# A chunked delta rule: zero rows under its 32-row operands, another order of its first products, its staging in three pieces

## What is computed

```python
H, DK, DV = (6, 32, 64)
beta = jax.nn.sigmoid(x @ Wb.T)
g = -jnp.exp(A_log) * jax.nn.softplus(x @ Wa.T + dt_bias)
q = l2norm(q) * DK ** (-0.5)
k = l2norm(k)

def step(S, inp):
    qt, kt, vt, gt, bt = inp
    S = S * jnp.exp(gt)[..., None, None]
    v_new = vt - jnp.einsum('bhk,bhkv->bhv', kt, S)
    S = S + bt[..., None, None] * (kt[..., :, None] * v_new[..., None, :])
    o = jnp.einsum('bhk,bhkv->bhv', qt, S)
    return (S, o)
_, o = jax.lax.scan(step, S0, (tm(q), tm(k), tm(v), tm(g), tm(beta)))
```

## Time and profile before

| | us |
|---|---|
| median of 3 runs | 3966.03 |
| lowest and highest run | 3959.83 and 3974.03 |
| the profiled execution | 3965.95 |
| its span in the trace | 3964.2 |
| mean granted TensorE clock | 0.933 |
| busy: PE, PEld | 3390.4 (86%), 2670.8 (67%) |
| busy: DVE, ACT, POOL | 2470.6 (62%), 1958.4 (49%), 1665.7 (42%) |
| `l2_delta_chunks` in the span | from 2142.8 to about 2523 |

### The profile page before, as it was taken

The page is one execution under the profiler, slowest core; times in us unless marked ns, Lnnn a source line. Parts: engine busy times, 40 slices in busy tenths (PEclk is TensorE's granted clock), DMA queues, the critical chain, the costliest instruction groups (busy, mean ns, idle before and its releaser), DMA issues. The chain is left out here.

```text
span 3964.2 us, 59001 instructions
## 1 busy us (share of the span) xinstructions
PE 3390.4 (86%) x18336; PEld 2670.8 (67%) x18336; DVE 2470.6 (62%) x4855; ACT 1958.4 (49%) x3947; POOL 1665.7 (42%) x1286
## 2 busy tenths in 40 slices
PE   5788698579888888879986999788888887998979
PEld 4566586158566666658874999656666666887868
DVE  4687544955577777775446444467777776545554
ACT  3777434333466666664333222256666664333333
POOL 1666221832466666642211433066666662221211
PEclk8899899999899999999997898799999998999989
DMA  2000232323110110003310000010000001332222
GB/s 79 18 29 2 76 110 64 133 95 108 46 29 25 25 29 23 19 19 119 111 62 5 1 1 1 34 41 23 23 23 25 25 16 61 114 109 85 80 88 75
DMA packets 81058, 203.12 MB, mean 51 GB/s; under 512 B 16923, under 2 KB 20123, under 8 KB 80662
## 3 DMA queue, kind: packets, MB, share of 16 engines
q1 hardware_dynamic: 80774, 201.26, 16.2%
q10 hardware_dynamic: 144, 0.07, 0.0%
HBM read 171.39 MB, written 4.69 MB: 44 GB/s over the span
## 5 line engine op out<-in xcount | busy, mean ns | idle before, releaser
L1209 POOL TENSOR_TENSOR probs<-probs,row_inverse 128x640 f32<-128x640 f32 (+7 forms) x640 | 733.1, 1147 | 593.7 <-DVE row_inverse L1235 576.2
L548 PE MATMUL psUp<-xnT_part,weights_part 128*128 128x512 f32 x3456 | 840.6, 393 | 3.3 <-DVE hidden L689 2.5
L548 PEld LDWEIGHTS psUp<-xnT_part,weights_part 128*128 128x128 f32 x3456 | 634.5, 189 | 125.9 <-POOL weights_part L522 3.3
L525 POOL TENSOR_TENSOR weights_part<-weights,weights_part 128x768 fp32r<-128x768 f32 x136 | 251.1, 1850 | 1028.3 <-ACT weights_part L598 1028.3
L1223 DVE TENSOR_REDUCE neg_max<-psS 128x1 f32<-128x640 f32 (+7 forms) x640 | 477.5, 746 | 160.3 <-PE psS L1114 160.2
L1192 ACT ACTIVATE probsT_part<-psT 128x512 fp32r<-128x512 f32 (+1 forms) x960 | 440.5, 490 | 270.0 <-PE psT L1126 268.5
L1250 DVE TENSOR_TENSOR probsT_part<-psT,probsT_part 128x512 fp32r<-128x512 f32 (+1 forms) x960 | 505.6, 552 | 103.7 <-ACT probsT_part L1192 87.0
L1126 PE MATMUL psT<-ident,probs 128*128 128x128 f32 x2880 | 452.7, 280 | 110.7 <-DVE probsT_part L1250 85.4
L1176 ACT ACTIVATE probs<-psS,neg_max 128x640 f32<-128x640 f32 (+7 forms) x640 | 474.9, 742 | 77.3 <-DVE neg_max L1223 72.4
L559 PEld LDWEIGHTS psDown<-weights_part,hidden_part 128*128 128x128 f32 x3456 | 461.6, 196 | 55.6 <-issue 23.3
L559 PE MATMUL psDown<-weights_part,hidden_part 128*128 128x256 f32 x3456 | 471.4, 288 | 31.0 <-DVE hidden_part L709 31.0
(11 more groups left out here) (318 smaller groups left out, 4922.6 us busy)
## 6 DMA issues: line engine op xcount, KB each, us to landing
gates<-gate_rows SPq DMA_DIRECT2D x136, 512.0 KB, 4.0
weights<-in_l_ffn SPq DMA_DIRECT2D x148, 384.0 KB, 4.4
qk_swapped<-qk_raw SPq DMA_DIRECT2D x384, 64.0 KB, 2.0
bc_broadcast<-bc_rows SPq DMA_DIRECT2D x32, 512.0 KB, 4.4
w_group<-in_l_wgroup SPq DMA_DIRECT2D x16, 384.0 KB, 3.2
q_whole<-q_steps SPq DMA_DIRECT2D x32, 128.0 KB
w_o_group<-in_l_wo SPq DMA_DIRECT2D x16, 256.0 KB, 2.6
rope<-in_l_rope SPq DMA_DIRECT2D x2, 1024.0 KB, 6.2
```

Of the source, the lines that this page charges most:

```text
L525: nc.gpsimd.tensor_tensor(w[1][:, j, :], wt[:, j, :], w[0][:, j, :].bitcast(F32), ALU.subtract).then_inc(w_split, 1)
L548: last = nc.tensor.matmul(psU[:, u % 2, g, :], wp[:, j, g * D + k * P:g * D + (k + 1) * P], xp[:, k, cols(half)], start=n == 0, stop=n == ...
L1209: self.nc.gpsimd.tensor_tensor(self.p[:, n % 4, 0:w], self.p[:, n % 4, 0:w], self.rinv[:, at:at + 1].to_broadcast([P, w]), ALU.mult).then_ ...
```

## The change

Six things change, all in the delta rule.

- `sT`, `rT` and `S` get 128 rows instead of 32 and move to `Delta`; POOL sets them to zero in `l2_delta_inputs`; ACT and DVE still write rows 0 to 31 only, and TensorE's products of them now run over 128 rows.
- POOL masks the L halves of all three banks first and the AT halves after them; L waits for its own half only (`l_masked`).
- On DVE, AT leaves `first` and becomes `attention`, done for the three banks behind `first(i, 2)`; `join(i, 0)` on TensorE waits for it (`a_done`) before it writes over that half of the bank.
- `turn_first` of the third bank stands behind `from_state(2i-1)` on TensorE.
- The mask of level 0 is negative, so that X = bs + I, with the operands in the other order.
- DVE's staging of the next pair comes in three pieces, behind levels 2, 3 and 4; the memset of `S` on DVE is gone.

```diff
--- before.py
+++ after.py
@@ Delta.__init__ @@
+        self.sT = s.sb("scaled_T", [P, 2, H, 4, P])
+        self.rT = s.sb("raw_T", [P, H, 4, P])
+        self.S = s.sb("state", [P, H, self.DV])
@@ l2_delta_inputs, gpsimd @@
             nc.gpsimd.memset(ones[:], 1.0).then_inc(const_set, 1)
+            for rows in (d.sT, d.rT, d.S):
+                nc.gpsimd.memset(rows[:], 0.0)
@@ l2_delta_chunks @@
-    sT = s.sb("scaled_T", [DK, 2, H, 4, P])
-    rT = s.sb("raw_T", [DK, H, 4, P])
+    sT, rT, S = d.sT, d.rT, d.S
...
-    S = s.sb("state", [DK, H, DV])
...
+    a_done = s.sem("attention_done")
+    l_masked = s.sem("l_decays_masked")
@@ gpsimd @@
                 for b in range(B):
                     pool.wait_ge(d_exp, B * i + b + 1)
-                    nc.gpsimd.tensor_tensor(ed[:, b, 0, :], ed[:, b, 0, :], flat(bm[:, b, :, :]), ALU.mult)
+                    nc.gpsimd.tensor_tensor(ed[:, b, 0, :], ed[:, b, 0, :], flat(bm[:, b, :, :]),
+                                            ALU.mult).then_inc(l_masked, 1)
+                for b in range(B):
                     nc.gpsimd.tensor_tensor(ed[:, b, 1, :].rearrange("p (s n) -> p s n", s=4),
                                             ed[:, b, 1, :].rearrange("p (s n) -> p s n", s=4),
                                             four(d.tri[:, 0, :]), ALU.mult).then_inc(masked, 1)
@@ tensor @@
             def turn(i):
-                pe.wait_ge(staged, i + 1)
+                pe.wait_ge(staged, 2 * i + 2)
...
-            def turn_first(i):
-                for b in range(B):
+            def turn_first(i, banks):
+                for b in banks:
...
                 for b in range(B):
                     pe.wait_ge(b_sb, level(i, k, b))
+                    if k == 0:
+                        pe.wait_ge(a_done, B * i + b + 1)
...
-                turn_first(i)
+                turn_first(i, range(B - 1))
                 if i:
                     from_state(2 * i - 1)
+                turn_first(i, range(B - 1, B))
                 join(i, 0)
@@ scalar @@
-                    nc.scalar.activation(flat(sT[:, i % 2, h, :, :]), ps[0:DK, 2 * (h % 3), :],
+                    nc.scalar.activation(flat(sT[0:DK, i % 2, h, :, :]), ps[0:DK, 2 * (h % 3), :],
                                          ACT.Copy).then_inc(st_done, 1)
-                    nc.scalar.activation(flat(rT[:, h, :, :]), ps[0:DK, 2 * (h % 3) + 1, :],
+                    nc.scalar.activation(flat(rT[0:DK, h, :, :]), ps[0:DK, 2 * (h % 3) + 1, :],
@@ vector @@
-            def stage(i):
-                for e in range(2):
-                    t = 2 * i + e
...
+            def stage(i, e):
+                t = 2 * i + e
...
                 last.then_inc(staged, 1)
+
+            def stage_logs(i):
                 for b in range(2):
                     nc.vector.tensor_tensor(lg[:, b, :, :], four(d.tri[:, 0, :]),
...
             def first(i, b):
-                dve.wait_ge(masked, B * i + b + 1)
+                dve.wait_ge(l_masked, B * i + b + 1)
                 dve.wait_ge(kq_ps, B * i + b + 1)
-                nc.vector.tensor_tensor(flat(L[:, b, :, :]), ps[:, 2 * b, :], ed[:, b, 0, :], ALU.mult)
-                nc.vector.tensor_tensor(flat(AT[:, i % 2, b, :, :]), ps[:, 2 * b + 1, :], ed[:, b, 1, :],
+                nc.vector.tensor_tensor(flat(L[:, b, :, :]), ps[:, 2 * b, :], ed[:, b, 0, :],
                                         ALU.mult).then_inc(la_done, 1)
...
-                nc.vector.tensor_tensor(X[:, b, :, :], four(ident[:]), bs[:, b, :, :],
-                                        ALU.subtract).then_inc(x0_done, 1)
+                nc.vector.tensor_tensor(X[:, b, :, :], bs[:, b, :, :], four(ident[:]), ALU.add).then_inc(x0_done, 1)
+
+            def attention(i, b):
+                dve.wait_ge(masked, B * i + b + 1)
+                nc.vector.tensor_tensor(flat(AT[:, i % 2, b, :, :]), ps[:, 2 * b + 1, :], ed[:, b, 1, :],
+                                        ALU.mult).then_inc(a_done, 1)
...
-            nc.vector.memset(S[:], 0.0).then_inc(s_done, 1)
-            stage(0)
+            stage(0, 0)
+            stage(0, 1)
+            dve.sem_inc(s_done, 1)
+            stage_logs(0)
...
                 first(i, 2)
+                for b in range(B):
+                    attention(i, b)
                 if i:
                     right_side(2 * i - 1)
...
                 for k in range(2, LEVELS):
                     join(i, k)
-                    if k == 3 and i + 1 < PAIRS:
-                        stage(i + 1)
+                    if 2 <= k < 4 and i + 1 < PAIRS:
+                        stage(i + 1, k - 2)
+                    if k == 4 and i + 1 < PAIRS:
+                        stage_logs(i + 1)
@@ host constants @@
-    out["l2_levels"] = np.ascontiguousarray(np.stack(join, axis=1).astype(np.float32))
+    levels = np.stack(join, axis=1).astype(np.float32)
+    levels[:, 0] *= -1.0
+    out["l2_levels"] = np.ascontiguousarray(levels)
```

More of the change, by code:

```diff
@@ L2486, in _ @@
         def _(dve):
-            def stage(i):
-                for e in range(2):
-                    t = 2 * i + e
[L2490 to L2494, removed]
+            def stage(i, e):
+                t = 2 * i + e
+                q3, k3 = (d.nat[:, t, lo:lo + HK].rearrange("p (h n) -> p h n", n=DK) for lo in (0, HK))
+                g3, k_end = (ap[:, t, :].unsqueeze(2).to_broadcast([P, H, DK]) for ap in (d.eg, d.ek))
+                for out, a, decay in ((sg[:, e, 0, :], q3, g3), (sg[:, e, 1, :], k3, g3),
+                                      (kd[:, i % 2, e, :], k3, k_end)):
+                    last = nc.vector.tensor_tensor(out.rearrange("p (h n) -> p h n", n=DK), a, decay, ALU.mult)
                 last.then_inc(staged, 1)
+            def stage_logs(i):
                 for b in range(2):
@@ L2529, in right_side @@
                 dve.wait_ge(s_done, n + 1)
-                nc.vector.tensor_tensor(Sd[:], S[:], d.ec[0:DK, n, :].unsqueeze(2).to_broadcast([DK, H, DV]),
+                nc.vector.tensor_tensor(Sd[:], S[0:DK], d.ec[0:DK, n, :].unsqueeze(2).to_broadcast([DK, H, DV]),
                                         ALU.mult).then_inc(sd_done, 1)
@@ L2541, in next_state @@
                 dve.wait_ge(sd_ps, n + 1)
-                nc.vector.tensor_tensor(flat(S[:]), flat(Sd[:]), ps[0:DK, 7, 0:H * DV], ALU.add).then_inc(s_done, 1)
-            nc.vector.memset(S[:], 0.0).then_inc(s_done, 1)
-            stage(0)
+                nc.vector.tensor_tensor(flat(S[0:DK]), flat(Sd[:]), ps[0:DK, 7, 0:H * DV], ALU.add).then_inc(s_done, 1)
+            stage(0, 0)
+            stage(0, 1)
+            dve.sem_inc(s_done, 1)
+            stage_logs(0)
             dve.wait_ge(masks_loaded, 16)
```

## The result

| | before | after |
|---|---|---|
| median, us | 3964.24 (4 runs, 3959.83 to 3974.03) | 3919.59 (4 runs, 3913.94 to 3925.86) |
| profiled execution, us | 3965.95 | 3922.23 |
| mean granted TensorE clock | 0.933 | 0.941 |
| `l2_delta_chunks`, first L2363 to the end of the last L2348, us | 374.3 | 328.5 |

The ratio of the runs is 0.9886, with a 95% interval from 0.9867 to 0.9905. The forecast was 3932, 34 us less, with a range from 3916 to 3954.

A forecast was written before the change was run, and what follows sets the result against it. A chain of stages bounds the kernel, with TensorE at half clock between products and level 0. Chain 31.1 - charge 3.9 + first pair 1.2 + staging 5.4 = 33.8 us, so 3966 - 34 = 3932; 8-in-10 range 3916 to 3954.

The forecast's parts named there:

- The zero rows hold the clock: In the products before level 0: 128 rows, 96 of them zero, should hold the high clock where 32 rows lose it.
- The new chain: From products to level 0: first L2409 16.4 us after the first product instead of 27.1; 31.1 us over three pairs.
- The charge for a clock that may still fall: Behind PE's 1.4 us idle for bank 2's X: 2.6 us a pair, charged in half the pairs, 3.9; bounds 0 to 7.8.
- Zero rows cost no time: In the products: 128 rows cost TensorE no time of their own; twelve records take 2.82 us against 2.66, both low.
- Staging: Behind levels 2 to 4: three pieces remove level 5's delay, 1.8 us three times, 5.4; bounds 4 to 5.4.
- The first pair: Before its level 0: two AT evictions leave DVE's chain, 1.2 us; the clock falls all the same; bounds 0.5 to 2.5.
- The tail: After the last pair: stays at clock 0.50, gain 0; at the high clock it would be 10 us shorter.
- The memsets: POOL zeroing 9600 columns from 2074.8: 10.3 us at a copy's rate, nobody waits, so 0.
- the slower rival: Memsets keep DVE from SBUF and delay the convolution; outweighs the gain from 5.1 ns a column, 3974 at 6 ns; chance 0.03.
- The forecast's own range: Whole time from 3924 (no falls, upper ends) to 3944 (falls in every pair, lower ends, DVE chain 1.5 us longer a pair).
- the one in which zero rows don't help: Products to level 0: clock still falls, order and staging alone give 12.6 us, time 3953; chance 0.22.
- The one in which the clock holds everywhere: Whole stage, tail included: high clock throughout, gain 47.7 us, time 3918; chance 0.13.

The follow-up runs named there:

- the 32-row run: The changed kernel with TensorE reading 32 rows of sT, rT and S again, everything else as changed: 3932.19 us, ratio 0.9918 to the kernel before.
- the filler run: The changed kernel with filler matmuls of 512 moving columns in the tail, written to banks nobody reads: 3914.05 us, ratio 0.9866 to the kernel before.
- the three runs built on it: The changed kernel with POOL's level 0 L mask behind X (3909.03 us), with tail fillers (3914.05), and with both plus AT masked in place behind level 1 (3904.86).

## Why the prediction was right, point by point

- **The zero rows hold the clock**: right. It stays at 1.00 from the products to level 0 in pairs 2 to 4, and the 32-row run shows that the rows do it. The rule of the Trainium skill that is cited there ("TensorE: Matmul & The Clock Gate", Part 1), by which busy time would set the clock, is not borne out here: 3.40 busy us of 3.40 with 32 rows and then half clock, before and in the run with the new order.
- **The new chain**: right, 16.4 us forecast and 16.0 measured. The third X was forecast to be done 12.8 us after the first product and was (2254.1 - 2241.33); B_level and X of bank 0 run against the maskings of AT as the sum had it.
- **The charge for a clock that may still fall**, 3.9 us: the step that was mis-sized. It did not fall in any of the three pairs, nor in the three of the filler run with the same stretch. The idle of 1.45 us among this work did not bring it down (6 of 6 pairs), those of 2.79 and 3.39 did (3 of 3 each). The charge was an even bet between two rows; its lower bound, 0, was the value.
- **Zero rows cost no time**: right in sign, too small. They give 2.2 us back: from level 0 to the next products it takes 60.9 us with 128 rows and 61.6 with 64 or 32 (56.0 against 56.3 in the first pair, 47.8 against 48.2 in the fourth). See the last section.
- **Staging**: 5.4 forecast, 5.8 measured alone.
- **The first pair**: 1.2 forecast, 2.5 measured, the upper bound. The rows have no part in it: the order with 32 rows gives 2.4 of it, the rows alone 0.1. Three AT evictions stood ahead of the third X, not two, and that X is done 1.5 us earlier behind the first product (12.7 instead of 14.2); 0.9 more comes from a clock that rises sooner within level 0 (L2409 4.01 us, L2402 4.92 before).
- **The tail**: 0 forecast, 2.7 measured. The clock falls 4.9 us into it, where it fell 2.9 us into it before; behind that it is as slow as it was. That later fall can't be put to the rows: with the same full rows and the same tail the clock fell after 3.2 us (rows alone) and 2.9 (transposes in their old place), and with 32 rows in the state's operands after 5.0 (rows for the products only). The tail took 25.9 and 26.1 us in the first two and 25.3 in the last. So full rows are worth about 1 us here (26.1 against 27.0 with the fall at 2.9, 24.3 against 25.3 with the fall at 5), and 1.7 us go with when the clock fell, which no run here explains. The bound of 10 us for a tail at the high clock was not reached by this change; with fillers the tail took 10.1 us less than in the kernel before.
- **The memsets** cost nothing: the first ends 5.22 us after it began, the three together take 8.3 us and are over at 2090.2, 7 us before DVE's next operation. The two large ones take 0.85 and 0.87 ns a column, against 5.1 needed for the slower rival. The sign of that rival, a `conv` behind 2092, came by the number (2098.1), but only because this whole execution runs some 7 us later: `conv` starts 16.3 us behind POOL's first memset of the stage (2081.80), 16.4 in the kernel before (2074.54 to 2090.95).
- **The forecast's own range**, 3924 to 3944, did not hold 3919.6. Nor is it the sum of the bounds given for its terms, which make 3927 to 3943: the tail and the rows' time had no bound of their own in it.

Of the rivals, the one in which zero rows don't help is excluded by the clock in the trace and by the run with 32 rows, where order and staging gave 17.0 us of the stage instead of the 12.6 put down for that rival. The one in which the clock holds everywhere came half true: in pairs 2 to 4, not in the first and not in the tail. The sum for it, 3918, is nearer to the measured 3919.6 than the forecast's 3932, but by another account, so its nearness is luck: 3.9 us of the charge, 2.7 in the tail, 2.2 from the rows and 1.3 in the first pair make, with 0.4 us of the chain in each of three pairs and 0.4 of the staging, the 12 us that the forecast lacked in the stage (45.8 against 33.8).

## What to carry to other kernels

Where TensorE is busy and its clock falls, look at how many rows the operands of each matmul have: here zero rows under operands of 32 rows kept the clock at 1.00 where it had fallen to 0.50, and matmuls that compute nothing paid off in a stretch of light ones (7.4 us). An idle of TensorE must be priced with the clock that it costs afterwards (4.4 us here for 1.3 us more of idle), so two edits of which one keeps the clock and the other shortens a wait can be worth more together than their sum (here 45.8 us against 35.5). And before an operand order or a broadcast is blamed for a slow VectorE operation with two SBUF inputs, look at what GpSimd does in that microsecond.

## What the runs showed of the hardware that I had not expected

Operands of fewer than 128 rows cost this kernel TensorE time even at the high clock. At clock 1.00, twelve records of q S with 64 moving columns and what follows them, first in the run with 64 rows, then in after:

```profile
2262.61 1.55 PE L2346 MATMUL ps<-state,scaled_T 64*128 64x64 f32 x12
2264.09 1.55 PE L2351 MATMUL ps<-u,AT 128*128 128x64 f32 x12
```

```profile
2272.06 1.45 PE L2346 MATMUL ps<-state,scaled_T 128*128 128x64 f32 x12
2273.35 1.50 PE L2351 MATMUL ps<-u,AT 128*128 128x64 f32 x12
```

From the start of L2346 to that of L2351 it is 1.48 us with 64 rows and, in the run with 32, the same 1.48 (2273.01 to 2274.49); with 128 rows it is 1.29. The twelve weight loads take 1.41 us with 32 rows and 1.42 with 128, so the loads themselves are no slower. In after the first load of the group starts 0.11 us before the first matmul, beside the work ahead of it, and in before it starts with it (2281.16 for both). It looks as if a load is not drawn ahead where the number of rows changes; no run here tests that by itself, so the cause stays open. The size is 0.2 us within a group of q S or k S and about 0.1 more where the number of rows changes beside it and at the start of the products, together 0.7 us a pair.

The second thing is that the clock does not need data in all rows: with zeros in 96 of 128 rows of both operands it held from the products to level 0 in pairs 2 to 4 of after and in the nine of the three runs built on it that keep its place for the transposes and its full rows. No run has data in all 128 rows of these operands, so whether that would count for more is open.
